# FFN activations of a gated cross-attention block: transposed by the DMA engines in 16 bits, with three PSUM banks for gate products and two for up

## The reference

```python
S      = (ctx @ Wq.T + bq) @ (ctx @ Wk.T + bk).T * H**-0.5
probs  = softmax(where(mask, -inf, S * layernorm(x)), axis=-1)
x      = x + tanh(g_xattn) * probs

quant_weight(w): s = mean(|w|) + 1e-5;             clip(round(w/s), -1, 1), s
quant_act(h):    s = max(|h|, last axis)/127+1e-5; clip(round(h/s), -128, 127), s
qlinear(h, w):   einsum of the two quantised arrays, times both scales

n = layernorm(x)
x = x + tanh(g_ffn) * qlinear(silu(qlinear(n, w_gate)) * qlinear(n, w_up), w_down)
```

## Time and profile before

| | |
|---|---|
| time, median of 3 runs | 255.97 us (255.76 to 256.09) |
| profiled execution: its own time | 255.76 us |
| its span in the profile | 254.0 us |
| mean granted TensorE clock | 0.94 of full speed |
| bytes moved by DMA | 22.89 MB |
| instructions | 3485 |

### The profile page before, as it was taken

One profiled execution on the slowest core, in us unless ns is written; L12 is line 12 of the kernel. 1 busy time (PEld: TensorE's weight loads), 2 busy tenths in 40 slices (PEclk: granted clock), 3 DMA queues, 4 the chain that ended last, 5 costly groups with the idle time before them and its releaser, 6 DMA issues.

```text
span 254.0 us, 3485 instructions
## 1 busy us (share of the span) xinstructions
PE 221.0 (87%) x1174; PEld 110.3 (43%) x1174; DVE 194.4 (77%) x356; ACT 165.8 (65%) x202; POOL 138.1 (54%) x191
## 2 busy tenths in 40 slices
PE   8700455989969899999999999999999999999994
PEld 6200152434424355544544544544544554445551
DVE  0699988897999789898988766879677851949621
ACT  2776958996985964447977437494963483754760
POOL 3975999998976998714297930310978400000000
PEclk9975555799999999999999999999999999999999
DMA  7999819960000010100011110000111101000112
GB/s 261 419 417 430 312 50 406 385 235 2 0 0 3 0 43 12 62 12 0 3 41 41 43 44 0 0 4 0 43 41 44 43 0 44 0 0 0 44 41 83
DMA packets 7041, 22.89 MB, mean 90 GB/s; under 512 B 624, under 2 KB 752, under 8 KB 5488
## 3 DMA queue, kind: packets, MB, share of 16 engines
q1 hardware_dynamic: 6880, 22.55, 22.8%
q10 hardware_dynamic: 144, 0.13, 0.2%
HBM read 18.48 MB, written 4.19 MB: 89 GB/s over the span
## 4 chain that ended last, share of the span: by engine, by line
PE 67%; POOL 15%; DVE 9%; issue 6%; DMA 2%; ACT 1%; SPq 0%; DVEq 0%; POOLq 0%
PE pD L900 22%; PE pU L870 18%; PE pG L857 17%; PE pT L888 5%; POOL stage_a L412 3%; POOL stage_b L412 3%; PE pA L835 3%; DMA hid<-in_masks 2%; POOL mask_bias L346 1%; DVE hid L1295 1%; POOL probs L381 1%; PE pA L845 1%; DVE st L1202 1%; DVE hid L1300 1%; POOL sd L371 1%
## 5 line engine op out<-in xcount | busy, mean ns | idle before, releaser
L619 ACT ACTIVATE hid<-pG,act_g 128x512 f32<-128x512 f32 x64 | 43.6, 687 | 37.8 <-PE pG L857 37.5
L857 PE MATMUL pG<-gate_w,xqT 128*128 128x512 bf16 x256 | 65.1, 387 | 1.8 <-ACT hid L619 1.1
L870 PE MATMUL pU<-up_w,xqT 128*128 128x512 bf16 x256 | 63.3, 379 | 3.7 <-DVE hid L1295 2.7
L900 PE MATMUL pD<-down_w,hidT 128*128 128x512 bf16 x256 | 58.7, 379 | 0.4 <-DVE stage_b L1323 0.4
L1295 DVE TENSOR_TENSOR hid<-pU,hid 128x512 f32<-128x512 f32 x64 | 43.6, 685 | 14.2 <-PE pU L870 11.6
L632 ACT ACTIVATE hidT<-pT 128x1024 bf16<-128x1024 f16 x32 | 32.2, 1020 | 20.6 <-PE pD L900 10.4
L870 PEld LDWEIGHTS pU<-up_w,xqT 128*128 128x128 bf16 x256 | 24.4, 98 | 36.0 <-DVE hid L1295 5.0
L419 POOL TENSOR_SCALAR out_scale<-den,act_u,down_k 128x1 f32<-128x1 f32 x16 | 6.4, 404 | 60.4 <-DVE den L1310 60.4
L857 PEld LDWEIGHTS pG<-gate_w,xqT 128*128 128x128 bf16 x256 | 24.7, 99 | 33.1 <-issue 6.0
L900 PEld LDWEIGHTS pD<-down_w,hidT 128*128 128x128 bf16 x256 | 24.5, 98 | 29.5 <-DVE stage_b L1323 0.7
L625 ACT ACTIVATE hid<-hid,magic_c,inv 128x1024 f32<-128x1024 f32 x24 | 29.4, 1237 | 4.1 <-DVE inv L1313 4.1
(11 more groups left out here) (103 smaller groups left out, 306.9 us busy)
## 6 DMA issues: line engine op xcount, KB each, us to landing
stage_a<-in_L_ffn_w_gate SPq DMA_DIRECT2D x4, 1024.0 KB, 10.4
stage_b<-in_L_ffn_w_up SPq DMA_DIRECT2D x4, 1024.0 KB, 18.8
stage_a<-in_L_ffn_w_down SPq DMA_DIRECT2D x4, 1024.0 KB, 5.8
stage_b<-in_x SPq DMA_DIRECT2D x2, 1024.0 KB, 5.8
out<-x SPq DMA_DIRECT2D x8, 256.0 KB, 2.0
out<-stage_b SPq DMA_DIRECT2D x8, 256.0 KB, 2.0
ctx_s<-in_ctx SPq DMA_DIRECT2D x4, 256.0 KB, 6.9
x<-in_x SPq DMA_DIRECT2D x2, 512.0 KB, 7.3
```

The costliest lines, as they stand in the source:

```text
L619: act.activation(hid[:, t % NH, n * 512:(n + 1) * 512], pG[n % 2][:, :], ACT.Silu, scale=act_g[:, t:t + 1]).then_inc(silu_done, 1)
L857: ins = pe.matmul(pG[n % 2][:, :], xqT[:, t // TILES % 2, t % TILES, k, :], gate_w[:, n, k, :], start=k == 0, stop=k == KD - 1)
L870: ins = pe.matmul(pU[n % 2][:, :], xqT[:, t // TILES % 2, t % TILES, k, :], up_w[:, n, k, :], start=k == 0, stop=k == KD - 1)
L900: ins = pe.matmul(pD[:, :], hidT[:, k, :], down_w[:, k // KD, k % KD, :], start=k == 0, stop=k == KI - 1)
```

## The change

- `transpose_hidden` leaves TensorE. A half is quantised with ROUND (1.5 x 2^23) in place of MAGIC, now by ScalarE in all 32 cases. A new step `hidden_16` takes ROUND off and writes bf16 into `hid16`, all 32 on GpSimd. SyncE issues one DMA transpose for each half from `hid16` to `hidT`, in an order among the stores. `copy_hiddenT` is gone.
- `hid16` and `hidT` have two slots each (t % 2). They lie in chunks 2 and 3 of `stage_b`, so the first two tiles wait for the up weights that were staged there.
- The two pT banks go: pG has three banks (c % 3, with c = 4t + n), pU two, pD two (t % 2), so down(t) waits for residual2(t-2).
- silu(t, 0) waits for `hidden_16` of tile t-4 instead of the transposes.
- Five weight chunks (gate 0 and 2, up 0 and 2, down 1) are no longer rounded by GpSimd: VectorE multiplies, takes the minimum with 1 and converts to int16 in one instruction, and takes the maximum with -1 in a second.
- Small column operations of VectorE (`exp_bias`, `gate_sums`, `inverse_x`, `inverse_hidden`) go from scalar_tensor_tensor over a group of columns to tensor_scalar, one for each column. GpSimd's `residual1` multiplies with rsum and tanh in one instruction.
- The orders of all engines are written anew. TensorE: `project_k(1)` comes before `transpose_x(0)`, which now waits for `k_ready`; down(12, 1) to down(15, 3) stand at the end behind all gate and up products.

```diff
@@
-        hidT = sb("hidT", [P, KI, P], BF16)
-        pG = [pb(f"pG{i}", [P, 512]) for i in range(2)]
-        pU = [pb(f"pU{i}", [P, 512]) for i in range(2)]
-        pT = [pb(f"pT{i}", [P, 512]) for i in range(2)]
-        pD = pb("pD", [P, 512])
+        pG = [pb(f"pG{i}", [P, 512]) for i in range(NG)]
+        pU = [pb(f"pU{i}", [P, 512]) for i in range(NU)]
+        pD = [pb(f"pD{i}", [P, 512]) for i in range(ND)]
+        hid16 = stage_b[:, 2, :].bitcast(BF16).rearrange("p (r i) -> p r i", r=2)
+        hidT = stage_b[:, 3, :].bitcast(BF16).rearrange("p (r k t) -> p r k t", r=2, t=P)
...
+        def short_free(engine, t, h):
+            if t >= 2:
+                engine.wait_ge(hidT_ready[t % 2][h], 16 * (t // 2))
+            else:
+                wait_ternary(engine, 1, 2)
...
-        ROUND_BY = ["PPPP", "PPPP", "PPPP"]
+        ROUND_BY = ["-P-P", "-P-P", "P-PP"]
@@ sync
+            def transpose_hidden(t, h):
+                wait_short(sp, t, h)
+                if t >= 2:
+                    sp.wait_ge(down_half, 2 * (t - 2) + h + 1)
+                else:
+                    wait_ternary(sp, 1, 3)
+                sp.dma_start_transpose(hidT[:, t % 2, 8 * h:8 * h + 8, :], hid16[:, t % 2, h * 1024:(h + 1) * 1024])\
+                  .then_inc(hidT_ready[t % 2][h], 16)
...
+            transpose_hidden(14, 0)
+            transpose_hidden(14, 1)
+            store(12)
+            transpose_hidden(15, 0)
+            transpose_hidden(15, 1)
+            store(13)
+            store(14)
+            store(15)
@@ gpsimd
+            def hidden_16(t, h):
+                short_free(pool, t, h)
+                wait_quantised(pool, t, h)
+                out16, part = short_args(t, h)
+                pool.tensor_scalar(out16, part, -ROUND, 1.0, ALU.add, ALU.mult).then_inc(h16_pool, 1)
...
-            weight_round(0, 0)
+            weight_round(0, 1)
             std2(0)
-            weight_round(0, 1)
-            weight_round(0, 2)
+            weight_round(0, 3)
+            gate_scales(0)
             centre(2)
-            weight_round(0, 3)
...
@@ scalar, start
+            act.wait_ge(consts, 6)
+            weight_sign(0, 1)
             weight_abs(1, 2)
+            weight_sign(0, 3)
+            quantise_x(0)
+            q_copy(1)
+            quantise_x(1)
             weight_abs(1, 3)
-            act.wait_ge(consts, 6)
-            quantise_x(0)
-            weight_sign(0, 1)
-            quantise_x(1)
-            weight_sign(0, 3)
-            q_copy(1)
+            k_copy(1)
             weight_abs(2, 0)
             weight_abs(2, 1)
             silu(0, 0)
@@ tensor
-                elif quarter == 0:
-                    pe.wait_ge(final_ready, t)
+                if quarter == 0:
+                    if t < ND:
+                        pe.wait_ge(scored, TILES)
+                    else:
+                        pe.wait_ge(final_ready, t - ND + 1)
                 if quarter % 2 == 0:
-                    pe.wait_ge(hidT_ready, 2 * t + quarter // 2 + 1)
+                    pe.wait_ge(hidT_ready[t % 2][quarter // 2], 16 * (t // 2 + 1))
...
@@ vector
             def weight_ternary(m, n):
                 chunk = ternary[m][:, n, :, :].rearrange("p k n -> p (k n)")
-                dve.tensor_scalar(chunk, stages[m][:, n, :], ROUND, 1.0, ALU.subtract, ALU.min).then_inc(w_upper, 1)
+                dve.wait_ge(winv_done, m + 1)
+                dve.tensor_scalar(chunk.bitcast(I16), stages[m][:, n, :], winv[:, m:m + 1], 1.0, ALU.mult, ALU.min)\
+                   .then_inc(w_upper, 1)
                 dve.wait_ge(w_upper, count(SIGN_BY, "V", m, n))
-                dve.tensor_scalar(chunk, chunk, -1.0, None, ALU.max).then_inc(w_ready_dve, 1)
+                dve.tensor_scalar(chunk, chunk.bitcast(I16), -1.0, None, ALU.max).then_inc(w_ready_dve, 1)
```

More of the change, by code:

```diff
@@ L26 @@
 NH = 4
+NG, NU, ND = 3, 2, 2
 WARM = 8
@@ L513, in _ @@
             residual1(8)
+            hidden_16(5, 0)
             residual1(9)
-            residual1(10)
-            std2(4)
-            residual1(11)
+            hidden_16(5, 1)
             centre(8)
             scale_out(6)
+            std2(4)
+            centre(9)
+            hidden_16(6, 0)
+            residual1(10)
+            hidden_16(6, 1)
+            quantise_x(8)
+            centre(10)
+            quantise_x(9)
+            gate_scales(4)
+            residual1(11)
+            up_scales(4)
+            hidden_16(7, 0)
             std2(5)
-            centre(9)
-            centre(10)
+            mask(14)
             centre(11)
[L524 to L527, removed]
+            mask(15)
+            hidden_16(7, 1)
             quantise_x(10)
@@ L532, in _ @@
             scale_out(7)
-            mask(14)
             scale_out(8)
-            mask(15)
+            hidden_16(8, 0)
+            hidden_16(8, 1)
             scale_out(9)
             residual1(12)
+            hidden_16(9, 0)
             residual1(13)
             centre(12)
-            residual1(14)
[L541 to L547, removed]
+            hidden_16(9, 1)
+            std2(6)
+            centre(13)
+            hidden_16(10, 0)
+            scale_out(10)
+            hidden_16(10, 1)
+            residual1(14)
             quantise_x(12)
@@ L551, in _ @@
             up_scales(6)
+            centre(14)
+            hidden_16(11, 0)
+            scale_out(11)
+            hidden_16(11, 1)
+            residual1(15)
+            std2(7)
+            centre(15)
+            scale_out(12)
             quantise_x(14)
             gate_scales(7)
+            hidden_16(12, 0)
+            up_scales(7)
             quantise_x(15)
-            up_scales(7)
-            scale_out(11)
-            scale_out(12)
+            hidden_16(12, 1)
             scale_out(13)
+            hidden_16(13, 0)
+            hidden_16(13, 1)
             scale_out(14)
+            hidden_16(14, 0)
+            hidden_16(14, 1)
             scale_out(15)
+            hidden_16(15, 0)
+            hidden_16(15, 1)
         @block.scalar
@@ L952, in _ @@
             up(1, 0)
+            gate(2, 2)
+            gate(2, 3)
+            project_k(2)
+            gate(3, 0)
             up(1, 1)
-            gate(2, 3)
-            gate(3, 0)
-            transpose_hidden(0, 0)
-            transpose_hidden(0, 1)
             up(1, 2)
             up(1, 3)
-            project_k(2)
             up(2, 0)
+            gate(3, 1)
             up(2, 1)
-            down(0, 0)
-            down(0, 1)
+            gate(3, 2)
             up(2, 2)
@@ L1137, in _ @@
             gate(12, 3)
-            transpose_hidden(11, 0)
-            transpose_hidden(11, 1)
+            up(12, 3)
             gate(13, 0)
+            up(13, 0)
             gate(13, 1)
+            up(13, 1)
+            gate(13, 2)
+            gate(13, 3)
+            up(13, 2)
+            up(13, 3)
             down(11, 0)
+            pe.wait_ge(xqT_ready, 7)
+            transpose_x(7)
             down(11, 1)
@@ L1224, in exp_bias @@
                 dve.wait_ge(rstd1_ready, g + 1)
[L1225 to L1226 removed]
+                for t in range(t0, t1):
+                    dve.tensor_scalar(negb[:, t:t + 1], mx[:, t:t + 1], rstd1[:, t:t + 1], -1.0, ALU.mult, ALU.mult)\
+                       .then_inc(negb_ready, 1)
             def gate_sums(g):
```

815 lines of the change are left out of this document (391 added, 424 removed).

## The result

The changed kernel takes 245.44 us (245.08 to 246.34), the kernel before 255.87 beside it: a ratio of 0.960, 95% interval 0.957 to 0.963. The forecast was faster, 239.5 us, range 232.5 to 250. The sign and the whole range held, but the time lies above the 244 at which the forecast's own case (A) ends: only the room that was left for rival (B) takes it in. 10.4 us came where 16.4 were expected. The profiled run took 246.34 us with a span of 244.6.

A forecast was written before the change was run, and what follows sets the result against it. TensorE was taken to bound from 77 us on, GpSimd's rounding and VectorE before. Span: 254.0 - 14.2 - 2.1 - 0.9 - 3 + 2 + 1.7 = 237.5 us, giving a time of 239.5, range 232.5 to 250.

The forecast's parts named there:

- case (A): The forecast itself, 239.5 us, with its own range of 232.5 to 244; chance 0.64.
- rival (B): VectorE, full in the head and nearly so until 140 us, becomes the bound for long: about 248; chance 0.18.
- The transposes' 14.2 us off TensorE: Removing TensorE's 256 transpose instructions shortens its path by 16 x 0.89 = 14.2 us, at least 13.4.
- behind products of later tiles: The new pass and DMA are hidden, as down(t) stands one to two tiles later in TensorE's new order.
- Prices of the pass and the DMA: GpSimd's hidden_16 takes 1.12 us a half; a DMA transpose of 256 KB takes 3 us, between 2.0 and 6.9.
- Rival C: The single queue of 32 transposes becomes the bound, from 5.5 us each; at 6.9 us the time is 300; chance 0.13.
- Transposes one after the other: DMA transposes on the SP queue run in sequence, each taking its full 3 us.
- the 1.7 us of stall: At the end, the last four transposes land after 12 us but are needed after 10.3: 1.7 us lost.
- 2.1 us earlier: In the head, TensorE's first gate product comes at 39.9 us, 2.1 us earlier.
- I take back 3 of the 9 us: In the head, fewer GpSimd rounds free VectorE and recover 3 of 9 us lost, bounds 0 and 7.
- The stalls in the middle and at the end: VectorE nearly full from 77 to 120 us adds 2 us; the last tiles' transposes add 1.7.
- The second down bank at nothing: The second pD bank removes a down's 0.4 us wait on the previous tile's residual; counted at nothing.

The follow-up runs named there:

- a7_round: The changed kernel with the int16 path undone, GpSimd rounding all twelve weight chunks again: 257.01 us, ratio 1.003.
- b1_dma: The kernel before with only the DMA transposes added, its orders, banks and weight path kept: 268.16 us, ratio 1.046.
- a1_warm: The changed kernel with TensorE's 16 warming passes moved ahead of project_k(1): 241.80 us, ratio 0.946.
- b2_int16: The kernel before with only the int16 path: VectorE converts five weight chunks, GpSimd rounds seven instead of twelve: 251.61 us, ratio 0.984.
- a6_tern: a1_warm with VectorE's weight_ternary(2, 1) moved behind product(1, 2): 241.15 us, ratio 0.942.
- a8_head: a6_tern with four more moves in the head, in the orders of VectorE, GpSimd and TensorE: 239.61 us, ratio 0.935.
- a3_pd1: The changed kernel with one down bank in use instead of two: 253.42 us, 8 us slower than changed.
- a5_whole: The changed kernel with one DMA transpose of 512 KB a tile in place of two of 256 KB: 259.70 us, ratio 1.015.

## Why the prediction came out as it did

- **The transposes' 14.2 us off TensorE**: right in place and size, but not by themselves. From 100 us on TensorE is full, and its work is shorter by them. The condition was in my text as a cover ("behind products of later tiles") and I gave it no price: in the old order it is missing, and the DMA transposes cost 12 us. a7_round is 11 us faster than b1_dma. It differs from it in the orders, the banks, the small operations and in that ScalarE does all quantisations of hidden halves (b1_dma leaves four each to GpSimd and VectorE). Of these only the second down bank was taken back alone; what the third pG bank, the small operations and the quantisations are worth no run shows.
- **Prices of the pass and the DMA**: 1.07 and 3.1 us for 1.12 and 3. The Trainium skill (Advanced Engine Details and Errata, X-Bar Transpose) states that on trn2 transposes by DMA are as fast as regular ones. The trace agrees only roughly: 3.1 us against 2.2 for a store of the same 256 KB. The Trainium skill (VectorE: DVE Perf Modes, The three transpose paths) gives 1309 ns for one block of 128x128. That figure does not add up over the blocks of one instruction: eight land in 3.1 us, sixteen in 4.3. Rival C, the slower side, falls with them.
- **Transposes one after the other**: wrong, and it did no harm. The sum took 3 us for each of the last four (the 1.7 us of stall), and rival C took 32 times the landing. But landings overlap: SyncE spends 1.23 us on an issue and goes on to the next, and in the changed kernel the last two, issued at 233.3 and 234.6 us, landed 3.2 and 3.1 us later, ahead of their downs; TensorE had no wait there.
- **The step that failed: the head.** "2.1 us earlier" became 0.45 later, 2.6 us off: 2.0 of it because I left the warming passes out of the chain (with them moved, a1_warm has its first gate 1.5 us earlier), 0.7 because the copy of k came later. "I take back 3 of the 9 us" became 5.3 us lost on top. That fewer rounds on GpSimd pay was sound in the old orders (4.3 us in all, b2_int16), but the new head has waits of TensorE of 10 us between 42 and 100 us where before had 6.4, one of 3.0 for a ternary chunk and one of 3.5 for a product, both from VectorE; and behind them TensorE works at the lower clock, for which my sum had no term. One row was also read too far: the 0.15 us of the instruction at L1272 "alone" is that at 31.12 us, which ran while GpSimd was in a weight round (30.64 to 33.04). The moves of a1_warm, a6_tern and a8_head together give 5.8 us back. That they end at the number forecast is chance: the 3.7 us of stalls in the sum did not come, and a8_head's head still loses about as much more than forecast.
- **The stalls in the middle and at the end** (2 + 1.7 us) were nearly absent: 1.0 us of waits from 100 us on, for a copy of x. Rival B is half true, as VectorE holds TensorE up in the head, and false after it. The 245.4 measured lie between the forecast and its 248.
- **The second down bank at nothing**: wrong, 8 us with the new order (a3_pd1). With both banks in place no wait for a residual is left from 77 us on, so the miss did not show in the total.

## What to carry to other kernels

A transpose moved from TensorE to the DMA engines takes work off the bound and puts latency into the chain of a tile (5.5 us from quantised half to down in b1_dma's longest wait, where TensorE and the copy took 1.5). It pays only with an order and banks that keep TensorE busy over it; here it cost 12 us in the old order, and the whole change, with new orders, banks and weight path, gave 10. When a term is freed by reordering, walk the new chain through every call between its ends, the warming ones too; count a wait of a few us with the slower clock that can follow it; and read a buffer's worth off the new order and not off the waits of the old.

## What the runs showed of the hardware

- A DMA transpose SBUF to SBUF of 128 x 1024 bf16: 1.23 us on the issuing queue in the median, landing in 3.1 us (3.0 to 5.7 in the changed kernel), and the next may be issued before it lands; of 128 x 2048: 1.3 to 2.9 us of issue and 4.2 to 5.0 to landing (a5_whole). The 32 of them raised the count of packets from 7041 to 40832, the new ones nearly all under 512 B.
- VectorE's f32 to int16 pass over 2048 columns took 1.28 to 2.38 us, the int16 to bf16 pass 0.69 to 2.35 (changed kernel). GpSimd was at work beside the short ones as well as the long ones, so what decides was not found out.
- The granted clock fell behind pauses of TensorE, and stayed at the lower level while it worked again: in the changed kernel 0.52 from 54 to 61 us, behind waits of 3.0 and 1.5 us, and 0.57 from 78 to 82, behind one of 3.5; in a5_whole, behind a pause of 4.4 us that ended at 88.4, 0.51 from 88 to 94. There TensorE worked 5.6 us, of which by an estimate (half of it) 2.7 are due to the clock. So a wait can cost more than its own length. Not each pause did this: a1_warm's waits of 1.7 and 1.5 us left the clock at 1.00.
